# The recurrent stage of a decoder kernel: decay as a matmul, joint additions and the quotient on POOL, three steps of lead, and the gate stored in two halves

## The reference, cut to what matters

```python
R, K, V = (time_interp(x, eps_i) @ W_i.T + b_i for each)          # 1024 channels each
W = -relu(time_decay) * (t - 1 - arange(t))
e = exp(clip(W + K, -20, 10));   eu = exp(clip(U + K, -20, 10))
A = shift(cumsum(e * V)) + eu * V
B = shift(cumsum(e)) + eu
out = (sigmoid(R) * (A / B)) @ Wo.T + bo
...
g = relu(einsum('bnmd,hd->bhnm', emb(boxes), Wg) + bg)            # emb: sin and cos
mn = softmax(log(clip(g, 1e-6)) + q k / 8)                        # cross attention
```

## Time and profile before

| | |
|---|---|
| median of 3 runs | 481.63 us (478.5 to 483.13) |
| the profiled execution | 481.88 us, its span 480.1 us |
| PE, DVE, ACT, POOL busy | 320.3, 335.9, 194.4, 90.0 us |
| mean granted clock of PE | 0.83 |
| DMA | 22500 packets, 16.91 MB |

### The profile page before, as it was taken

One profiled execution on the slowest core, in us unless ns is written; L12 is line 12 of the kernel. 1 busy time (PEld: TensorE's weight loads), 2 busy tenths in 40 slices (PEclk: granted clock), 3 DMA queues, 4 the chain that ended last, 5 costly groups with the idle time before them and its releaser, 6 DMA issues.

```text
span 480.1 us, 8901 instructions
## 1 busy us (share of the span) xinstructions
PE 320.3 (67%) x3651; PEld 197.5 (41%) x3651; DVE 335.9 (70%) x479; ACT 194.4 (40%) x310; POOL 90.0 (19%) x86
## 2 busy tenths in 40 slices
PE   2605779767666575799999973920095998789821
PEld 0201233222222334477777761400033777467710
DVE  0796899999999955666666644488833674666574
ACT  1519968546445330122222252475113442434420
POOL 0070033444343403400000000000003341112000
PEclk9856799888899597699999996765576798989965
DMA  8600000000005768100000000000000000000001
GB/s 236 255 0 16 1 1 22 23 22 22 1 21 101 132 117 286 73 3 1 3 1 3 3 1 0 0 0 1 0 0 0 3 4 3 1 2 5 3 0 44
DMA packets 22500, 16.91 MB, mean 35 GB/s; under 512 B 17216, under 2 KB 20416, under 8 KB 22336
## 3 DMA queue, kind: packets, MB, share of 16 engines
q1 hardware_dynamic: 22464, 16.39, 12.5%
HBM read 11.67 MB, written 4.72 MB: 34 GB/s over the span
## 4 chain that ended last, share of the span: by engine, by line
PE 36%; DVE 19%; SPq 6%; issue 5%; ACT 3%; DMA 1%; POOL 0%; DVEq 0%; ACTq 0%; POOLq 0%
PE psum L441 29%; SPq L423 6%; PE psum L699 3%; DVE small L1455 2%; DVE arena_a L1397 2%; PE psum L581 2%; PE psum L548 2%; DVE small L1539 1%; DVE arena_a L1417 1%; ACT arena_b L1050 1%; DMA g_scratch<-arena_a 1%; DVE arena_b L1510 1%; DVE arena_b L1516 1%; DVE arena_b L1543 1%; DVE xc L1220 1%
## 5 line engine op out<-in xcount | busy, mean ns | idle before, releaser
L441 PE MATMUL psum<-arena_b 64*64 64x9 f32 (+2 forms) x1348 | 75.3, 278 | 43.8 <-DVE arena_b L1364 30.6
L441 PEld LDWEIGHTS psum<-arena_b 64*64 64x64 f32 (+2 forms) x1348 | 34.9, 141 | 73.6 <-issue 38.8
L441 PE MATMUL psum<-arena_a 64*64 64x64 f32 (+2 forms) x1056 | 34.8, 235 | 9.0 <-ACT arena_a L904 5.4
L1539 DVE TENSOR_REDUCE small<-psum 128x16 f32<-128x1024 f32 x16 | 19.6, 1225 | 20.2 <-PE psum L441 20.2
L441 PEld LDWEIGHTS psum<-arena_a 64*64 64x64 f32 (+1 forms) x1056 | 21.9, 139 | 28.5 <-issue 15.8
L1148 POOL TENSOR_TENSOR arena_b<-arena_b 128x512 f32<-128x512 f32 x16 | 24.8, 1551 | 43.3 <-DVE arena_b L1334 43.3
L441 PE MATMUL psum<-arena_a,xw 128*128 128x128 f32 x256 | 31.1, 279 | 2.4 <-ACT arena_a L969 2.2
L441 PEld LDWEIGHTS psum<-arena_a,xw 128*128 128x128 f32 x256 | 30.1, 195 | 4.0 <-ACT arena_a L969 2.7
L441 PE MATMUL psum<-arena_b,const 32*128 32x128 f32 (+1 forms) x138 | 9.1, 346 | 32.3 <-DVE arena_b L1462 32.0
L1172 POOL MEMSET arena_b<- 128x16 f32 x4 | 0.3, 128 | 160.1 <-DVE x L1529 160.1
L1145 POOL TENSOR_TENSOR arena_b<-arena_b 128x512 f32<-128x512 f32 x16 | 21.9, 1369 | 44.0 <-DVE arena_b L1351 44.0
(11 more groups left out here) (218 smaller groups left out, 731.1 us busy)
## 6 DMA issues: line engine op xcount, KB each, us to landing
g_scratch<-arena_a SPq DMA_DIRECT2D x16, 256.0 KB, 6.6
logg<-g_scratch SPq DMA_DIRECT2D x1, 3584.0 KB, 13.2
xw<-in_xw SPq DMA_DIRECT2D x1, 2048.0 KB, 9.1
arena_b<-in_rkvo SPq DMA_DIRECT2D x8, 192.0 KB, 2.3
ffn_w<-in_ffn SPq DMA_DIRECT2D x1, 576.0 KB, 10.8
x<-in_xT SPq DMA_DIRECT2D x2, 256.0 KB, 3.0
arena_a<-in_boxes SPq DMA_DIRECT2D x8, 64.0 KB, 4.0
arena_b<-in_rkvo SPq DMA_DIRECT2D x8, 64.0 KB, 1.9
```

Source lines behind the costliest of these rows:

```text
L441: return nc.tensor.matmul(o, l, r, start=start, stop=stop, **kw)
L1539: v_.tensor_reduce(mx.rearrange("p (r h) -> p r h", r=4), s4, axis=AX.X, op=ALU.max).then_inc(s.a_max, 1)
```

## The change

- The steps are written out for each engine in turn, with no loop. Three buffers for w_rkv and for the terms (`terms`: e, eu, e v, eu v in one tile), four for w_o and for y_sb, three for `sums`, two for `div`.
- Decay: z on DVE is gone. ACT takes eu from the k bank first; then PE adds `decay_row` (1 partition) times t_rem to the same bank (`r_decay`), and ACT takes e from it. POOL prepares decay_row once.
- k runs three steps ahead of r, v two, decay two. k, v and e, eu alternate banks as before; r has one bank, and the other bank of pC holds the scan mask, which DVE writes with two memsets at the start.
- ACT writes exp(-r) back into the bank, then adds 1 (`r_er1`); the clip to 2**43 and the product with the sum are one DVE operation (`r_divisor`).
- DVE: clip, product, both scans of the same step, the divisor of the step before. POOL: one addition of 1024 columns for both sums, and the quotient y (the last two steps' quotients on DVE).
- The box products: four in each of steps 1 to 4, relus of one bank on DVE and of the other on ACT, one logarithm in each of steps 2 to 9. The output products of steps 0 to 3 come together in step 5.
- SP stores the gate in two halves of 16 transfers of 128 KB. Its whole order stands in the diff. Tiles 0 to 3 are loaded after the first half, 4 to 7 after the second; DVE waits for the latter at tile 4.
- Behind the stage: the layer norm of half 0 and x_k, x_keys of tile 0 ahead of the last quotient, the operations on the feed-forward weights ahead of x_queries.

```diff
-        def run_chunks(eng, step):
...
+            def weights_rkv(ch):
+                if ch >= 3:
+                    sp.wait_ge(s.r_psum, 2 * (ch - 2))
+                    sp.wait_ge(s.v_psum, 2 * (ch - 2))
+                sp.dma_start(w_rkv[ch % 3], rkvo[ch, :, 0:384]).then_inc(s.w_in[ch % 3], 16)
+            def weights_o(ch):
+                if ch >= 4:
+                    sp.wait_ge(s.o_acc, 2 * (ch - 3))
+                sp.dma_start(w_o[ch % 4], rkvo[ch, :, 384:512]).then_inc(s.wo_in[ch % 4], 16)
...
+            def store_g(f):
+                sp.wait_ge(s.g_log, 4 * f + 4)
+                for hd in range(H):
+                    at = 4096 * (hd // 8) + 2048 * f
+                    sp.dma_start(by_half[f, 8 * (hd % 2) + hd // 2], g_sb[16 * (hd % 8):16 * (hd % 8) + 16, at:at + 2048]
+                                 .rearrange("p (k m) -> p k m", m=S)).then_inc(s.g_out, 16)
+            for ch in range(3, 5):
+                weights_rkv(ch)
+            weights_o(4)
+            store_g(0)
+            weights_rkv(5)
+            weights_o(5)
             sp.wait_ge(s.g_out, 16 * 16)
             sp.dma_start(logg[:, 0:1], by_tile[:, 0:1]).then_inc(s.g_in0, 16)
-            sp.dma_start(logg[:, 1:TILES], by_tile[:, 1:TILES]).then_inc(s.g_in, 16)
+            sp.dma_start(logg[:, 1:4], by_tile[:, 1:4]).then_inc(s.g_in, 16)
+            weights_rkv(6)
+            weights_o(6)
+            store_g(1)
+            weights_rkv(7)
+            weights_o(7)
+            sp.wait_ge(s.g_out, 32 * 16)
+            sp.dma_start(logg[:, 4:8], by_tile[:, 4:8]).then_inc(s.g_in1, 16)
...
+            def r_k(n):                       # PE
+                if h == 0:
+                    pe.wait_ge(s.w_in[ch % 3], 16 * (ch // 3 + 1))
+                if n < 2:
+                    pe.wait_ge(s.mix_done, 3 * h + 3)
+                else:
+                    pe.wait_ge(s.e_done, n - 1)
+                mm(half(pA, h), w_rkv[ch % 3][:, 128:256], half(x_mix[1], h)).then_inc(s.k_psum, 1)
+            def r_decay(n):
+                pe.wait_ge(s.eu_done, n + 1)
+                mm(half(pA, h), decay_row[:, ch * P:(ch + 1) * P], rows(c("t_rem")[0:1], 8), start=False,
+                   skip_group_check=True).then_inc(s.w_psum, 1)
...
+            for n in range(RWKV_STEPS):
+                r_r(n)
+                if n + 2 < RWKV_STEPS:
+                    r_v(n + 2)
+                if n + 3 < RWKV_STEPS:
+                    r_k(n + 3)
+                if 1 <= n < 5:
+                    box_product(4 * n - 4, 4 * n)
+                if n == 5:
+                    for j in range(4):
+                        r_out(j)
+                if n > 5:
+                    r_out(n - 2)
+                if n >= 1 and n + 2 < RWKV_STEPS:
+                    r_decay(n + 2)
+            r_out(RWKV_STEPS - 2)
...
+            r_eu(0)                           # ACT
+            r_eu(1)
+            r_e(0)
+            r_e(1)
+            r_eu(2)
+            r_e(2)
+            r_er(0)
+            r_er1(0)
+            box_sines()
+            for n in range(1, RWKV_STEPS):
+                r_inverse(n - 1)
+                r_er(n)
+                if n + 2 < RWKV_STEPS:
+                    r_eu(n + 2)
+                r_er1(n)
+                if n < 5:
+                    box_relu(2 * n - 2)
+                    box_relu(2 * n - 1)
+                if n + 2 < RWKV_STEPS:
+                    r_e(n + 2)
+                if LOG_STEPS <= n < LOG_STEPS + 8:
+                    log_g(n - LOG_STEPS)
+            r_inverse(RWKV_STEPS - 1)
...
+            def r_add(n):                     # POOL
+                pool.wait_ge(s.sum_done, n + 1)
+                two = sums[n % 3].rearrange("p (a t) -> p a t", a=2)
+                g.tensor_tensor(two, two, pairs[n % 3][:, :, HALF + 1:], ALU.add).then_inc(s.ab_done, 1)
+            def r_y(n):
+                pool.wait_ge(s.d_inv, n + 1)
+                pool.wait_ge(s.ab_done, n + 1)
+                if n >= 4:
+                    pool.wait_ge(s.o_acc, n - 3)
+                g.tensor_tensor(y_sb[n % 4], sums[n % 3][:, HALF:], div[n % 2], ALU.mult).then_inc(s.y_done, 1)
+            for n in range(RWKV_STEPS):
+                r_add(n)
+                if 1 <= n < RWKV_STEPS - 1:
+                    r_y(n - 1)
...
+            for n in range(RWKV_STEPS):       # DVE
+                r_terms(n)                    # clip, product with v
+                r_sums(n)                     # two scans
+                if 2 <= n < 6:
+                    box_relu(2 * n - 4)
+                    box_relu(2 * n - 3)
+                if n >= 1:
+                    r_divisor(n - 1)
+            r_y(RWKV_STEPS - 2)
+            r_divisor(RWKV_STEPS - 1)
+            residual1(0)
+            dve.wait_ge(s.x1_done, 1)
+            r_y(RWKV_STEPS - 1)
```

More of the change, by code:

```diff
@@ L61, with build_program @@
     pass
-def build_program(nc, xT, ctxT, boxes, rkvo, par_in, const_in, xw_in, ffn_in, l1_in, out, g_scratch):
+def build_program(nc, xT, ctxT, boxes, rkvo, decay, par_in, const_in, xw_in, ffn_in, l1_in, out, g_scratch):
     with ExitStack() as ctx:
@@ L116, in build_program @@
         feat = cg(4096)
-        wg_spread = cg(4160)[:, 0:256]
+        wg_spread = cg(256)
+        cg(832)
+        sums = [cg(1024) for _ in range(3)]
         g_sb = cg(8192)
@@ L379, in run_tiles @@
                 step(t, t % 2, t > 0, t < TILES - 1)
-        def run_chunks(eng, step):
[L383 to L388, removed]
+        scan_mask = half(pC, 1)
         @block.sync
@@ L956, in _, with log_g, r_eu @@
-            run_chunks(act, rwkv)
+            def log_g(k):
+                cc, i = k % 2, k // 2
+                act.wait_ge(s.g_relu_act if cc else s.g_relu_dve, 2 * i + 2)
+                g_two = g_sb[:, (8 * cc + 2 * i) * HALF:(8 * cc + 2 * i + 2) * HALF]
+                nc.scalar.activation(g_two, g_two, ACT.Ln, bias=der[:, 28:29]).then_inc(s.g_log, 1)
+            act.wait_ge(s.par_in, 16)
+            act.wait_ge(s.par_set, 4)
+            def r_eu(n):
+                ch, h = n // 2, n % 2
+                act.wait_ge(s.k_psum, n + 1)
+                if n >= 3:
+                    act.wait_ge(s.ab_done, n - 2)
+                nc.scalar.activation(e_eu[n % 3][:, HALF:], half(pA, h), ACT.Exp, bias=der[:, 8 + ch:9 + ch])\
+                    .then_inc(s.eu_done, 1)
@@ new lines, in r_sums, with r_divisor @@
+            def r_sums(n):
+                dve.wait_ge(s.ev_done, n + 1)
+                if n >= 3:
+                    dve.wait_ge(s.y_done, n - 2)
+                for i in range(2):
+                    last = v_.tensor_tensor_scan(sums[n % 3][:, i * HALF:(i + 1) * HALF], pairs[n % 3][:, i, 0:HALF],
+                                                 scan_mask, 0.0, ALU.add, ALU.mult)
+                last.then_inc(s.sum_done, 1)
+            def r_divisor(n):
+                dve.wait_ge(s.er1_done, n + 1)
+                dve.wait_ge(s.ab_done, n + 1)
+                if n >= 2:
+                    dve.wait_ge(s.y_done, n - 1)
+                v_.scalar_tensor_tensor(div[n % 2], half(pC, 0), 2.0 ** 43, sums[n % 3][:, 0:HALF], ALU.min, ALU.mult)\
+                    .then_inc(s.d_done, 1)
```

372 lines of the change are left out of this document (144 added, 228 removed).

## The result

The changed kernel takes 500.46 us (median of 4 executions, 495.57 to 503.12), the kernel before, on the same chip, 480.4 us (478.5 to 483.13): ratio 1.0378, 95% interval 1.0298 to 1.0458. It is slower by 18 us (by the ratio) to 20 us (by the medians); 498 was forecast. The profiled execution is the quickest of the four: 495.57 us, span 494.0, granted clock 0.841 (the others: spans 498.6 to 501.6, clocks 0.809 to 0.819). So two traces compared give 13.9 us, the medians 20. All ratios leave out executions over 1.5% above the quickest of their kernel.

A forecast was written before the change was run, and what follows sets the result against it. Bound: DVE at 6.95 us per step, then the gate's store. The first score scaling moves from 187.0 to 203.6, +16.6; 480.1 + 16.6 = 496.7 span, plus 1.8: 498 us, own range 487 to 509, overall 471 to 509.

The forecast's parts named there:

- The cause: SP's order: weights of chunks 5 and 7 stand behind the gate's stores, so k(10) and k(14) stall PE.
- without a stall: Rival: weight loads come in time or stores issue quickly; first score scaling at 177.8, 472.7 us in all; chance 0.12.
- with a short one: Rival: partly held, weights land 8 us after their issue is wanted; about 484 us; chance 0.07.
- with 31 us a half: Rival: the store costs 2.03 us per transfer, not per piece, each stall 31 us; 530 us; chance 0.03.
- The store: SP's gate store: 15.3 us of issue per half, weights behind it landing 20.5 us after the half's first issue.
- the tail of 5.8 us: After a half's last store issue: the queue drains about 5.8 us more, and a weight load behind it lands with that.
- The stalls: Recurrent stage: PE waits at k(10) for chunk 5, 15 us, and at k(14) for chunk 7, another 14 us.
- The steps: Steady recurrent steps: 6.2 us against 6.95, the clip waiting 1.4 us for POOL's addition; ends 5.0 and 7.2.
- The pair of rows that this rested on: DVE's L1328 in two rows: 0.46 us when POOL is idle, 1.31 beside POOL's addition, ending 0.28 after it.
- Head and box steps: Start of the stage: ACT reaches step 1 at 69, ten us later; four box steps of 8.65 us; clip(7) at 108.4.
- Behind the stage: From the end of y(15) to the first score scaling: 9.3 us, bounds 8 and 11.7; all that follows unchanged at 293 us.

The follow-up runs named there:

- a_order: The changed kernel with SP's order alone changed, the weights of chunk 5 issued ahead of the first half's stores, chunk 7 ahead of the second: 480.12 us, ratio 0.9971.
- c_short_add: a_order with POOL's joint addition over 16 of its 1024 columns: 470.69 us, ratio 0.9769.
- j_ffn_slots: a_order with first box relu before scans, r(0) and sines earlier, feed-forward quantisation in the head, POOL's first operation of it behind step 0's addition: 465.64 us, ratio 0.9682.
- e_clip_psum: a_order with DVE's first box relu ahead of the scans and one operand of the clip in PSUM: 475.64 us, ratio 0.9864.

## Why the prediction was right, step by step

**The cause: shown.** SP's order, a store ahead of chunks 5 and 7, and a gap on PE behind each. a_order undoes that alone and takes away 20 us of 20. The rivals without a stall, with a short one and with 31 us a half fell with the profile after (both gaps, 14.39 and 13.88 us of issue).

**The store: right in kind, some 3 us long.** Forecast: 15.3 us of issue for a half, weights 20.5 after the first issue, from 109.5. Measured: first issue at 110.73, 14.39 of issue (0.89 median for one transfer, against 2.03 for one of twice the pieces), weights landed 17.8 after the first issue, 17.2 in the second half: just under the quick end of the bounds (18). The step that was off is the tail of 5.8 us: a load of other data issued behind the backlog lands after 3.3 us, where it takes 2.3 alone. The 5.8 of the earlier trace rows was the wait for the stores' own landings, not a queue that the weights have to sit out: a store of 256 KB landed 5.1 to 8.1 us after its issue, one of 128 KB takes 3.0 to 3.9.

**The stalls: 15 and 14 forecast, 10.1 and 8.7 on PE, 12.6 and 9.8 on DVE.** Chunk 5 was wanted at 118.4, not 115.2. PE had fallen to its lower level just before, with pairs of 1.88 to 1.91 us; I had counted the low clock only after the gaps. That delay cost nothing by itself, as PE would have waited anyway.

**The steps: 6.2 forecast, 6.4 to 6.75 measured** (from product to product). A clip that is ready at once takes 2.13 us beside an addition of 2.00 and 2.50 beside one of 2.37; I had taken 2.07. One that comes later takes less (1.47 to 2.18), with the same end. c_short_add shows that all of it is POOL's addition. The pair of rows that this rested on was misread: L1328 at 81.08 isn't a case of an idle POOL.

```profile
79.86 1.39 POOL L1145 TENSOR_TENSOR arena_b<-arena_b 128x512 f32<-128x512 f32 x1 [1.52 <-DVE arena_b L1351]
```

That addition ended at 81.25 and L1328 at 81.54, 0.29 us later, as the other one ended 0.28 after its addition. Both were held, so 0.46 is no undisturbed length; the rule of the wait came out right all the same. And the 4.24 us for terms and scans are 4.33 by the spacings in the earlier trace rows, 4.37 measured (75.47 to 79.84). The Trainium skill (SBUF — State Buffer, section "SBUF: two separate sides") says that the shared pair is an exclusive lock, held for a whole instruction by whichever of the two engines began, where DVE needs it for an operation in a 2-port mode or with two SBUF inputs. The traces agree: the clip ends 0.55 us after POOL's addition in each step where it is held, and a quotient that POOL begins behind a waiting clip takes 1.72 us instead of 1.27; so do j_ffn_slots and the clip with a PSUM operand.

**Head and box steps.** ACT at step 1: 69 forecast, 66.9 measured; clip(3) 75.4 against 75.47, because PE's pairs behind it were at the lower level: two errors of about 2 us cancelled. Box step 8.65 against 9.0. Clip(7) 108.4 against 109.77. What came before a weight load's landing was absorbed by it, so the end of y(15) is the second landing (166.8 forecast, 163.0 measured) and what follows it (27.5 and 30.0): 194.3 against 193.0. That this is so close is luck: the weights landed 5 us sooner behind their stores than forecast, over both halves, and the compute between and behind the landings 3.5 us slower.

**Behind the stage: a term mis-sized, hidden by another.** From y(15) to the first scaling 9.3 was forecast (bounds 8 and 11.7) and 16.8 measured, outside the bounds. The failed step is a term that the sum left out: the section on the change says that the operations on the feed-forward weights move ahead of x_queries, and the prediction puts no price on that and leaves POOL's part in tile 0. POOL's rounding, which they release, now falls on the norm's second product (4.03 for 0.69 us), and PE, idle meanwhile, does the scores behind it at the lower level:

```profile
207.66 1.98 PE L447 MATMUL psum<-arena_a 64*64 64x64 f32 x64 [3.64 <-DVE xn L1286]
```

In j_ffn_slots, where the operations lie in the head, these are 0.69 and 1.16 us, and the scaling comes 12.6 after y(15). So 4.2 of the 7.5 missing are the stop (3.4 of POOL, 0.8 of PE's clock); DVE's own 1.9 us cost nothing, as the second product starts 10.5 us after y(15) in both. The other 3.3 are the work moved ahead of y(15), which bought nothing: the scores end 12.4 after y(15) even in j_ffn_slots, against 11.7 before, since on PE the second half's norm products now stand behind those of x_k and x_q.

The same stop used to be inside tile 0 (L1417, 4.75 us, and PE's products behind it at the lower level), so the second scaling follows after 9.5 instead of 15.8, which I had left at "a microsecond". From there to the end the same instructions take 274.7 instead of 277.3 us, at a granted clock of 0.86 instead of 0.83, which the forecast did not have. The forecast's 293.1 us from the first scaling to the end were thus 284.2. Together: -1.3 + 7.5 - 8.9 = -2.7, which is 496.7 against 494.0. Again luck: the terms behind the stage were 7 to 9 us off in both directions.

**The number.** 498 against a median of 500.46, and 495.57 for the profiled execution. The right sum of the trace was a little under the forecast; the median lies above it, and the other three executions had a lower clock (0.809 to 0.819).

**The rival without a stall** was put at 472.7. a_order, which is that case, has 480.1. In its trace y(15) ends at 174.9 instead of 168.5 (longer box steps, longer steady steps, steps at the lower clock), +6.4; the first scaling follows after 16.8 instead of 9.3, +7.5; from there to the end are 287.2 instead of 293.1, -5.9. So the change's own gain was overrated by 7 to 8 us; it only didn't matter beside the stalls.

## What to carry to other kernels

A queue is a place in the schedule: before a block of stores goes into an in-order queue, ask which load stands behind it, when that is wanted, and which in-order engine stops with it; here two moved lines are 20 us. Work given to POOL isn't free for DVE when DVE has an SBUF operation ready beside it: count POOL's whole instruction as DVE's, or put it where DVE waits for something else (j_ffn_slots), or try DVE's operation with an operand in PSUM. When a shortened step brings nothing, look at PE's pairs too: here steps of c_short_add and e_clip_psum were lost to pairs of 1.9 us instead of 1.02. And before two traces are compared at a late instruction, compare them at one that stands ahead of every edit.

## What I had not expected of the hardware

- POOL's rounding of 128x1152 (add, subtract) takes 4.10 us in every kernel, with DVE busy or idle beside it, the next operation of the same kind and shape (min, max) 1.15 us, or 1.65 beside DVE. The decay's operation on one partition (max, multiply; 1x1024) takes 3.63, as the rounding some 3.6 ns a column. Why is open.
- DVE's clip of 128x1024 with a PSUM operand takes 1.22 us for 0.67 alone, and is still cheaper than 2.13 beside POOL.
- POOL's addition takes 2.00 us in some steps and 2.36 in others of the same kernel. It is 2.35 to 2.37 in steps 1, 4, 7, 10 and 13 of every kernel that has it whole, those that use the second of the three buffers, and 2.00 in the rest but step 0. So it goes with the buffer; what about the buffer sets it, no run shows.
